# A two-layer graph transformer on one core: masked scores stay in PSUM, GpSimd divides, and the output projection stands between the halves of the second MLP product

## The reference

```python
# layer 0: 8 heads of 32
nx = ln(x, ln1_g, ln1_b)
q, k, v = (heads(nx @ w + b) for w, b in ((wq, bq), (wk, bk), (wv, bv)))
bias = where(adj > 0, 0.1 * adj * adj, -inf)
attn = softmax(q @ k.T / sqrt(32) + bias)
x1 = x + (attn @ v) @ wo + bo
x = x1 + gelu(ln(x1, ln2_g, ln2_b) @ w1 + b1) @ w2 + b2      # w1: 256 x 1024
# layer 1: one head of 256
sc = where(adj == 0, -inf, (x @ Wq) @ (x @ Wk).T / 16)
y = x + (softmax(sc) @ (x @ Wv)) @ Wo + bo1
out = ln(y, gamma, beta)
```

## Time and profile before

| | |
|---|---|
| median of three runs | 961.03 us (959.05 to 961.2) |
| the profiled execution | 959.66 us, of which its span on the engines 957.8 us |
| granted TensorE clock, mean | 0.982 |
| TensorE busy | 863.9 us (90%) |
| VectorE busy | 725.0 us (76%) |
| ScalarE busy | 618.6 us (65%) |
| GpSimd busy | 387.9 us (41%) |

### The profile page before, as it was taken

One profiled execution on the slowest core, in us unless ns is written; L12 is line 12 of the kernel. 1 busy time (PEld: TensorE's weight loads), 2 busy tenths in 40 slices (PEclk: granted clock), 3 DMA queues, 4 the chain that ended last, 5 costly groups with the idle time before them and its releaser, 6 DMA issues.

```text
span 957.8 us, 21811 instructions
## 1 busy us (share of the span) xinstructions
PE 863.9 (90%) x7159; PEld 764.6 (80%) x7159; DVE 725.0 (76%) x2638; ACT 618.6 (65%) x1830; POOL 387.9 (41%) x258
## 2 busy tenths in 40 slices
PE   8987698989999898999999989998998989898996
PEld 7876488787878878788787878878787877888896
DVE  7686849599595968959597795959869595977645
ACT  6785666667576666757567565757756666684642
POOL 4534034525345452434535244453524445262412
PEclk9898799999999999999999999999999999999999
DMA  7100432524133242514324241342423224242000
GB/s 254 34 1 2 120 112 66 160 67 139 43 99 120 66 142 66 153 33 107 123 66 142 66 122 64 84 146 66 133 71 101 89 71 154 55 133 74 38 23 34
DMA packets 106304, 87.11 MB, mean 91 GB/s; under 512 B 3463, under 2 KB 91165, under 8 KB 106269
## 3 DMA queue, kind: packets, MB, share of 16 engines
q1 hardware_dynamic: 106252, 86.66, 29.9%
q10 hardware_dynamic: 16, 0.00, 0.0%
HBM read 47.85 MB, written 38.80 MB: 90 GB/s over the span
## 4 chain that ended last, share of the span: by engine, by line
PE 39%; DVE 35%; issue 15%; ACT 5%; POOL 3%; DVEq 1%; DMA 0%; POOLq 0%; SPq 0%; ACTq 0%
PE bank L398 10%; PE bank L400 9%; PE bank L399 9%; DVE p_s L1292 6%; DVE stats L1243 4%; DVE p_s L1302 4%; PE bank L581 3%; DVE nx L1260 3%; PE bank L714 3%; DVE nxT_lo L1184 2%; DVE x L1366 2%; PE bank L559 2%; DVE pT L1312 2%; POOL rstd L1693 2%; DVE x L1334 2%
## 5 line engine op out<-in xcount | busy, mean ns | idle before, releaser
L1292 DVE CUSTOM_DVE_ANT_0 p_s<-bank,bias 128x128 f32<-128x128 f32 x512 | 112.4, 284 | 140.7 <-PE bank L559 140.6
L950 ACT ACTIVATE bank<-p_s,neg_max 128x128 f32<-128x128 f32 x512 | 182.6, 357 | 44.5 <-DVE neg_max L1292 44.5
L398 PE MATMUL bank<-w_hi,hT_hi 128*128 128x256 f32 x512 | 146.2, 286 | 1.3 <-DVE hT_lo L1184 1.3
L400 PE MATMUL bank<-w_hi,hT_lo 128*128 128x256 f32 x512 | 144.2, 282 | 0.0
L399 PE MATMUL bank<-w_lo,hT_hi 128*128 128x256 f32 x512 | 144.0, 281 | 0.0
L1768 POOL TENSOR_TENSOR x<-x,bo_r 128x1024 f32<-128x1024 f32 (+1 forms) x16 | 37.3, 2333 | 234.0 <-PE bank L664 234.0
L398 PE MATMUL bank<-n2T_hi,w_hi 128*128 128x512 f32 (+1 forms) x272 | 111.2, 409 | 20.0 <-DVE hT_lo L1184 20.0
L1693 POOL TENSOR_TENSOR rstd<-ve,minus_half 128x4 f32<-128x4 f32 (+1 forms) x49 | 49.8, 1017 | 184.3 <-DVE ve L1253 184.1
L981 ACT ACTIVATE bank<-bank,vec_cols 128x512 f32<-128x512 f32 (+1 forms) x136 | 86.7, 637 | 33.4 <-PE bank L400 27.6
L400 PE MATMUL bank<-n2T_hi,w_lo 128*128 128x512 f32 (+1 forms) x272 | 105.1, 387 | 0.0
L399 PE MATMUL bank<-n2T_lo,w_hi 128*128 128x512 f32 (+1 forms) x272 | 105.0, 386 | 0.0
(11 more groups left out here) (229 smaller groups left out, 2356.9 us busy)
## 6 DMA issues: line engine op xcount, KB each, us to landing
parked<-pT SPq DMA_DIRECT2D x116, 256.0 KB, 4.0
pT<-parked SPq DMA_DIRECT2D x15, 1024.0 KB, 5.5
p_s<-parked SPq DMA_DIRECT2D x14, 1024.0 KB, 7.7
xs<-in_x SPq DMA_DIRECT2D x15, 512.0 KB, 3.8
out<-y SPq DMA_DIRECT2D x14, 512.0 KB, 3.0
adj_i<-in_adj SPq DMA_DIRECT2D x15, 256.0 KB, 2.8
out<-y SPq DMA_DIRECT2D x3, 256.0 KB, 2.2
x2T_f<-in_L_gnn_w SPq DMA_DIRECT2D x1, 512.0 KB, 6.8
```

The lines of the kernel that those rows point to most:

```text
L398: mm(out, a_hi, b_hi, start=first, stop=False)
L400: return mm(out, a_lo, b_hi, start=False, stop=last)
L950: last = run(bank[r][:, NODES * place:NODES * place + NODES], p_s[:, r, place, :], ACT.Exp, scale=-1.0, bias=neg_max[:, r, place:place + 1 ...
L1292: last = V.tensor_tensor_reduce(p_s[:, r, place, :], bank[r][:, NODES * place:NODES * place + NODES], bias0[:, 2 * q + place // 2, :], -1. ...
```

## The change

Groups 0 and 1 keep the old way. For all others:

- `biased` writes the masked scores back into their PSUM bank instead of `p_s`, and `exps` reads the bank and writes `p_s`. The bank is free once the exponentials are done, so `scores` of the second half and the next group's transposes wait for ScalarE instead of VectorE's division.
- `divided` is split. VectorE keeps the reciprocal (`inverse`); GpSimd multiplies `p_s` in place (`normal`), eight times in a whole turn, and the transposes wait for GpSimd.
- TensorE's order: the second MLP product is no longer begun ahead of attention. Its first half stands behind the first scores, the two output projections behind that, then the second scores, the second half of the product, v, and x2's transposes directly ahead of `t_project`. `scores1` gets PSUM bank 5 instead of 7 and stands behind the first `vo_project`.
- ScalarE, VectorE, GpSimd and SyncE get new orders. SyncE stores and loads the second half in the turn that computed it, not in the next.

```diff
-
...
+            def turn(gp, gc):
                 if not is_last(gp):
                     load_adj(gp + 1)
                 store(gc)
                 store_blocks(gp, 0)
                 if not is_last(gp):
                     load_x(gp + 1)
-
-            turn(3, 2, 0)
+                    store_blocks(gp, 1)
+                for q in pairs(gp):
+                    load_blocks(gp, q)
...
@@ -544,7 +547,7 @@
                     pe.wait_ge(act_q, 2 * g + 2)
                 if by_blocks(g):
                     if q == 1:
-                        pe.wait_ge(dve_p, 4 * pair0(g) + 4)
+                        pe.wait_ge(act_p, 4 * pair0(g) + 4)
                     elif isinstance(g, int) and g == 2:
                         pe.wait_ge(dve_x1, pair0(g))
...
@@ -734,21 +738,20 @@
                 project_k(gp, 1)
                 project_q(gp, 0)
                 project_q(gp, 1)
-                mlp_down(gb, 0, (0,))
                 attend(ga, 0)
                 attend(ga, 1)
                 scores(gp, 0)
-                mlp_down(gb, 0, (1,))
-                mlp_down(gb, 1)
+                mlp_down(gb, 0)
+                out_project(ga, 0)
+                out_project(ga, 1)
                 if size(gp) > 2:
                     scores(gp, 1)
+                mlp_down(gb, 1)
+                project_v(gp, 0)
                 x2_transpose(gb)
-                out_project(ga, 0)
-                out_project(ga, 1)
                 t_project(gb)
-                project_v(gp, 0)
-                scores1(gb, True)
                 vo_project(gb, 0, True)
+                scores1(gb)
                 vo_project(gb, 1, True)
                 n2_transpose(ga, True)
                 p1_transpose(gb)
...
@@ -946,8 +949,15 @@
             def exps(g, q, r):
 
                 act.wait_ge(dve_s, 4 * (pair0(g) + q) + r + 1)
+                if by_blocks(g):
+                    if q == 1:
+                        act.wait_ge(dve_blocks, blocks_done(g, 0, r))
+                    elif r == 0:
+                        act.wait_ge(pe_av, pair0(g))
                 for place in range(4):
-                    last = run(bank[r][:, NODES * place:NODES * place + NODES], p_s[:, r, place, :], ACT.Exp, scale=-1.0,
+                    scored, part = bank[r][:, NODES * place:NODES * place + NODES], p_s[:, r, place, :]
+                    to, of = (part, scored) if by_blocks(g) else (scored, part)
+                    last = run(to, of, ACT.Exp, scale=-1.0,
                                bias=neg_max[:, r, place:place + 1], accum_out=psum[:, r, place:place + 1])
                 last.then_inc(act_p, 1)
...
@@ -1284,26 +1293,29 @@
                 dve.wait_ge(pe_s, pair0(g) + q + 1)
                 if q == 0 and r == 0:
                     dve.wait_ge(pool_bias, g + 1)
-                    dve.wait_ge(pe_av, pair0(g))
-                if q == 1 and by_blocks(g):
-                    dve.wait_ge(dve_blocks, blocks_done(g, 0, r))
+                    if not by_blocks(g):
+                        dve.wait_ge(pe_av, pair0(g))
                 dve.sem_inc(stand_dve, 1)
                 for place in range(4):
+                    scored = bank[r][:, NODES * place:NODES * place + NODES]
                     last = V.tensor_tensor_reduce(
-                        p_s[:, r, place, :], bank[r][:, NODES * place:NODES * place + NODES],
+                        scored if by_blocks(g) else p_s[:, r, place, :], scored,
                         bias0[:, 2 * q + place // 2, :], -1.0, -3.0 * MASKED, ALU.add, ALU.min, neg_max[:, r, place:place + 1])
                 last.then_inc(dve_s, 1)
 
+            def inverse(g, q, r):
+                dve.wait_ge(act_p, 4 * (pair0(g) + q) + r + 1)
+                V.reciprocal(rsum[:, r, :], psum[:, r, :]).then_inc(dve_r, 1)
+
             def divided(g, q, r):
                 count = 4 * (pair0(g) + q) + r + 1
-                dve.wait_ge(act_p, count)
-                V.reciprocal(rsum[:, r, :], psum[:, r, :]).then_inc(dve_r, 1)
+                inverse(g, q, r)
                 dve.wait_ge(dve_r, count)
                 V.tensor_tensor(p_s[:, r, :, :], bank[r][:, :].rearrange("p (h n) -> p h n", h=4),
                                 rsum[:, r, :, None].to_broadcast([128, 4, NODES]), ALU.mult).then_inc(dve_p, 1)
 
             def blocks(g, q, r):
-                dve.wait_ge(dve_p, 4 * (pair0(g) + q) + r + 1)
+                dve.wait_ge(pool_p, blocks_done(g, q, r))
                 if r == 0:
...
@@ -1457,62 +1469,60 @@
                 sums1(gp)
                 moments(1, gp)
                 h_low(gb, 0)
+                norm1(gp)
+                for j in range(1, 5):
+                    h_low(gb, j)
                 sums3(gc)
-                norm1(gp)
-                h_low(gb, 1)
-                h_low(gb, 2)
+                nxT_low(gp)
                 moments(3, gc)
-                h_low(gb, 3)
+                h_low(gb, 5)
+                h_low(gb, 6)
+                h_low(gb, 7)
                 norm3(gc)
-                h_low(gb, 4)
-                nxT_low(gp)
-                for j in range(5, HT):
-                    h_low(gb, j)
+                attn_low(ga, 0)
+                attn_low(ga, 1)
                 for r in range(HPT):
                     biased(gp, 0, r)
-                attn_low(ga, 0)
-                divided(gp, 0, 0)
+                inverse(gp, 0, 0)
+                inverse(gp, 0, 1)
+                inverse(gp, 0, 2)
                 blocks(gp, 0, 0)
-                divided(gp, 0, 1)
+                inverse(gp, 0, 3)
+                residual2(gb, 0)
                 blocks(gp, 0, 1)
-                residual2(gb, 0)
-                divided(gp, 0, 2)
-                divided(gp, 0, 3)
-                attn_low(ga, 1)
                 blocks(gp, 0, 2)
-                residual2(gb, 1)
                 blocks(gp, 0, 3)
+                residual1(ga, 0, True)
+                residual1(ga, 1, True)
                 if whole:
                     biased(gp, 1, 0)
                     biased(gp, 1, 1)
-                x2T_low(gb)
-                residual1(ga, 0, True)
-                if whole:
                     biased(gp, 1, 2)
-                residual1(ga, 1, True)
+                residual2(gb, 1)
                 if whole:
                     biased(gp, 1, 3)
+                    inverse(gp, 1, 0)
+                    inverse(gp, 1, 1)
                 sums2(ga, 0)
                 sums2(ga, 1)
+                if whole:
+                    inverse(gp, 1, 2)
+                    blocks(gp, 1, 0)
+                x2T_low(gb)
+                if whole:
+                    inverse(gp, 1, 3)
+                    blocks(gp, 1, 1)
                 moments(2, ga)
+                if whole:
+                    blocks(gp, 1, 2)
                 t_copy(gb)
                 if whole:
-                    divided(gp, 1, 0)
-                    blocks(gp, 1, 0)
+                    blocks(gp, 1, 3)
                 norm2(ga)
                 biased1(gb)
-                if whole:
-                    divided(gp, 1, 1)
-                    blocks(gp, 1, 1)
                 vo_copy(gb)
-                if whole:
-                    divided(gp, 1, 2)
-                    blocks(gp, 1, 2)
                 n2T_low(ga)
                 inverse_sums1(gb)
-                if whole:
-                    divided(gp, 1, 3)
-                    blocks(gp, 1, 3)
                 residual3(gb, 0)
                 residual3(gb, 1)
...
@@ -1562,13 +1572,17 @@
                 n2T_low(1)
                 inverse_sums1(0)
                 for r in range(HPT):
-                    divided(2, 0, r)
-                    blocks(2, 0, r)
+                    inverse(2, 0, r)
+                blocks(2, 0, 0)
+                blocks(2, 0, 1)
+                for r in range(HPT):
+                    biased(2, 1, r)
+                blocks(2, 0, 2)
+                blocks(2, 0, 3)
                 residual3(0, 0)
                 for r in range(HPT):
-                    biased(2, 1, r)
+                    inverse(2, 1, r)
                 for r in range(HPT):
-                    divided(2, 1, r)
                     blocks(2, 1, r)
...
 
+            def normal(g, q, r):
+                pool.wait_ge(dve_r, 4 * (pair0(g) + q) + r + 1)
+                P.tensor_tensor(p_s[:, r, :, :], p_s[:, r, :, :], rsum[:, r, :, None].to_broadcast([128, 4, NODES]),
+                                ALU.mult).then_inc(pool_p, 1)
...
             def turn(gp, ga, gb, gc):
                 rstd(1, gp)
                 pool.wait_ge(ln_dve[1], ln_end(gp))
-                if gc is not None:
-                    rstd(3, gc)
                 adjacency(gp)
                 edges(gp)
                 bias(gp)
-                if gc is not None:
-                    gain(gc, size(gc))
-                    offset(gc, size(gc))
-                x2_plus_bo(gb)
+                rstd(3, gc)
```

(19 more changed lines are left out.)

84 lines of the change are left out of this document (51 added, 33 removed).

## The result

The changed kernel takes 1004.66 us (median of 4 runs, 1003.24 to 1005.68); the kernel before took 960.12 beside it. The ratio is 1.046, with a 95% interval of 1.044 to 1.048. The forecast was 955, with a range of 938 to 970: the kernel became slower instead of faster, and lies outside the range.

A forecast was written before the change was run, and what follows sets the result against it. It took a cycle through TensorE's projections, attention and scores, then some 45 us of VectorE, as the bound. Thirteen turns -7.8, first turn +1.0, short group -0.3, clock +1.2: 959.66 becomes 953.8, 955 on the medians' scale; range 938 to 970.

The forecast's parts named there:

- Until the first exponential: From k's projection to the first mask: projections, attention and attn_low end at 9.15 us; GpSimd's bias is early enough.
- the divisions: Eight 128x512 divisions a turn on GpSimd: first at 12.7 us, keeping up with ScalarE's exponentials, with 0.6 us to spare.
- what TensorE does meanwhile: TensorE's work up to x2's transposes ends at 27.0 us; it then waits 2.6 us until t_project at 29.6.
- The divisions' size: One 128x512 division on GpSimd taken at 1.30 us, with a lower end of 1.2 and an upper end of 2.05.
- The exponentials and x2: ScalarE's exponentials from PSUM to SBUF: change taken as 0, bounds 0.04 us each way; t_project starts at 29.6 us.
- 948 us: Time if the skill's fixed cycles alone held: each exponential saves 43 ns, twelve 0.5 us a turn, 6.7 us in all.
- From t_project to the next zero: Rest of the turn, from t_project to the next k's projection: 28.46 us before, 26.1 forecast, making the turn 55.7.
- GpSimd sets the turn: Rival: slower divisions on GpSimd hold up the turn; at 1.62 us each the time is 967 us; chance 0.14.
- The clock falls each turn: Rival: TensorE's clock falls in all 13 turns at 0.9 us, 11.7 instead of 1.2, giving 965 us; chance 0.16.
- The small terms: Corrections outside the 13 repeated turns: +1.0 us in the first turn, -0.3 in the short group's turn.
- first turn's +1.0: In the first turn VectorE's transposes are done 1.0 us later, so TensorE's wait of 6.54 us ends 1.0 later.
- The short group's turn: Turn of the last, short group: x2's wait, 2.7 us before, stays near 2.4, a gain of 0.3 us.

The follow-up runs named there:

- the wait back: The changed kernel with GpSimd's wait for the end of norm2 put back between LayerNorm 2's rstd and the additions x2_plus_bo and x1_plus_b2: 943.72 us, ratio 0.9835.
- masks in SBUF: Against the changed kernel with GpSimd's norm2 wait restored: VectorE writes masked scores to SBUF, exponentials go SBUF to SBUF, divisions stay on GpSimd: 943.73 us.

## Why the prediction was wrong

By its own steps:

- **Until the first exponential, the divisions, what TensorE does meanwhile: right.** The first mask was forecast at 9.15 and came at 9.01 (490.12 - 481.11), t_project at 29.6 and came at 29.50, the wait for x2T_lo at 2.6 and came at 2.56 on average (38.4 in 15). This held for every kernel with this order and the divisions on GpSimd.
- **The divisions' size: a row too high.** 1.30 us taken, 1.04 measured (four in 4.04), under my lower end of 1.2. They hardly held anything up: VectorE's transposes waited 1.3 us for them in the whole run.
- **The exponentials and x2.** Taken at 0, which the time bears out, but by luck: I had let the destination take back what the source gives. The exponentials gained 43 ns each (0.344 us apart instead of 0.3875, and 0.387 from SBUF to SBUF), and the masks lost 38. The Trainium skill, "VectorE: DVE Perf Modes", section on the errata of SBUF sources, has these 43 ns, and the trace agrees. The net on the time is next to nothing, because twelve quicker exponentials end in a wait for v. So the 948 us that I had derived from that rule would not have come.
- **From t_project to the next zero: the step that failed.** It was summed to 26.1 and is 30.2. I let x_bo and rstd stand ahead of norm2 and gave norm2 the 402 ns of the earlier trace rows, so that the mask would be done at 37.7. norm2 started as forecast (516.46 - 481.11 = 35.35), but the mask was done only at 41 (522.06 - 481.11). With the wait back this stretch takes 25.05, 1.05 better than my sum: without a collision the forecast was too high, not too low (I had summed 1.2 us of waits in it, the trace has 0.4). 25.05, 2.2 of standing and 3.0 of slower matmuls make the 30.2. The layout missed that the change drops GpSimd's wait for norm2 and puts 4.8 us of additions exactly there. I had priced only what stands ahead of rstd, not what was queued behind it.
- **The clue was in my own rows, misread.** I took the 504 ns of y's norm against 402 for a slowdown by a quarter. In one turn of the kernel before, the four are 559, 403, 699 and 402 ns: single ones are held, others not at all. The first of them, and the third with the second:

```profile
L1260 DVE TENSOR_SCALAR y<-y,mv,rstd x1: 559/559/559, 459.5 to 459.5; 128x256 f32<-128x256 f32 x1
...
L1260 DVE TENSOR_SCALAR y<-y,mv,rstd x2: 403/551/699, 459.9 to 460.3; 128x256 f32<-128x256 f32 x2
```

  GpSimd was at a cast (459.27 + 0.61) and then at a two-step `TENSOR_SCALAR` (460.07 + 2.07), which did not hold them for its length. No row of before had one of GpSimd's additions beside a norm: the wait kept them apart. But the size could have been read elsewhere in it. In the short group's turn a `TENSOR_SCALAR` of 128x2, whose line has a median of 170 ns, took 1.62 us and ended with GpSimd's addition of LayerNorm 3's offset (910.31 and 910.28):

```profile
907.90 2.38 POOL L1778 TENSOR_TENSOR y<-y,beta_r 128x1024 f32<-128x1024 f32 x1
...
908.69 1.62 DVE L1253 TENSOR_SCALAR ve<-mv 128x2 f32<-128x2 f32 x1
```

  A glance at the longest `TENSOR_SCALAR` instead of the mean would have given it. The Trainium skill, "SBUF — State Buffer", section "Who interferes with whom", states the size: "Whoever issues first gets the shared pair for the whole instruction; the other **fully blocks** (not throttle)". It says so of VectorE's modes that use both of its port pairs, which it lets `tensor_scalar` enter under conditions; for forms with two SBUF inputs it gives contention with a GpSimd instruction that reads SBUF; and an instruction with at most one SBUF input outside those modes it calls free of it. The norms beside additions agree (up to 2466 and 2598 ns), and so do transposes from SBUF (692 ns on average while GpSimd divided, 708 before). Which mode the norms ran in no run here shows. GpSimd's `TENSOR_SCALAR` above does not fit so simply, and no run here settles why.
- **The rivals.** "GpSimd sets the turn" named the right pair of engines at the wrong place, the divisions, and gave 967; slower came true, but not by its reason. "The clock falls each turn" came true as a consequence, and twice in each turn: with the same wait for x2T_lo and no second wait the clock stayed at 1.00, so that wait alone, which I had blamed, doesn't do it. The clock more than doubles the price of the collision: 2.2 us standing, 3.0 at half clock.
- **The small terms.** The first turn's +1.0 did not come: TensorE's wait ahead of the MLP went from 6.54 to 6.1 us. Its own terms already gave only 0.1: 3.5 later, and 2.6 instead of four times 1.5, which is 3.4 shorter. The short group's turn was to gain 0.3: its wait for x2 went from 2.7 to 2.6 us, not to 2.4, and from its first k's projection to the end of the span it is 101.3 us before, 102.5 in the changed kernel and 103.4 with the wait back. All this is small against the 45 us.

The three parts, each undone on the kernel with the wait back: divisions on GpSimd earned 42 us, masks in PSUM 0, TensorE's order 2. They overlap, so they need not add. Together they make the kernel 16 us faster than before; the missing wait takes 61, which leaves the loss of 45.

Open: why the 2.7 us for x2T_lo bring a fall in some turns (the first two and the short group's with the wait back, two late ones with masks in SBUF) and not in others, and why waits of at most 1.4 us brought one in ten turns of the kernel before without its wait.

## What to carry to other kernels

A semaphore wait for which no data is exchanged may be there to keep two engines apart: before one is dropped, list what will then run beside what, and look at the longest single instruction, not the mean, of both. Long GpSimd instructions belong where VectorE transposes (692 ns) or reads PSUM (with the wait back, the masks of layer 1 beside an addition take 0.28 us, as without one), or cut in pieces; a norm whose result TensorE waits for belongs alone. And standing that is added on TensorE can cost twice its length, here 5.2 us a turn for 2.2, so a forecast should price a second wait in the turn higher than the first.

## What the runs showed of the hardware

- GpSimd's product of 128x512 with a value spread over each 128 elements takes 1.04 us, less than its product of two tensors of that size (1.29).
- VectorE's mask with its result in PSUM takes 325 ns against 285 in SBUF. ScalarE's exponentials show a longer row from PSUM to SBUF (397 against 357) but start 0.344 us apart against 0.3875: the rows overlap, and the distance of starts is the price.
- A tiny `TENSOR_SCALAR` of 128x4 is held as well: 1.19 us in the changed kernel beside GpSimd's 1.29 us sum for the bias, 0.17 to 0.22 elsewhere.
